# Layer 1 of a four-layer FFN kernel: the router's columns are pooled together with x, and the pooling's steps are reordered

## The reference, cut to what matters

```
attn_in = tanh(x @ W1 + b1)                  # (2, 1024, 64)
scores  = attn_in @ v                        # (2, 1024)
mask    = prefix, suffix, or all but itself, by prompt_type_ids[b]
p       = softmax(where(mask, scores, -1e30))          # (2, 1024, 1024)
z       = (p @ x) / count(mask)              # pooled rows
logits  = z @ Wr + br                        # (2, 1024, 8)
expert  = argmax(logits);  gate = softmax(logits)[expert]
out     = x + gate * FFN_expert(z)
```

## Time and profile before

| what | us |
|---|---|
| runs | 1240.93, 1246.62, 1247.62 |
| the profiled execution | 1239.08 |
| its span | 1237.2 |
[...]
| TensorE matmul busy | 1078.8 |
| VectorE busy | 931.1 |
| ScalarE busy | 647.5 |
| GpSimd busy | 505.1 |

### The profile page before, as it was taken

How to read it: one execution, slowest core, us unless ns; L and a number is a source line. 1 busy time by engine, 2 the same in 40 slices (tenths; PEclk the granted TensorE clock), 3 DMA queues, 4 the chain that set the end, 5 groups by cost and what they waited for, 6 DMA issues and landing times.

```text
span 1237.2 us, 25849 instructions
## 1 busy us (share of the span) xinstructions
PE 1078.8 (87%) x7880; PEld 1004.0 (81%) x7880; DVE 931.1 (75%) x1603; ACT 647.5 (52%) x1370; POOL 505.1 (41%) x345
## 2 busy tenths in 40 slices
PE   6689867999999999999997666999868968989896
PEld 4478857999999999999995446999758966778785
DVE  6766795888888888888865856887547866767695
ACT  3335315767667677676744436676246735323221
POOL 5000013778887888887851004453116750000000
PEclk8799987999999999999996777999889988999898
DMA  6300227676777777777633115764346854030202
GB/s 181 118 21 4 76 85 258 187 244 206 253 233 224 244 224 243 229 224 256 211 63 77 35 52 222 286 215 148 113 162 196 269 163 158 30 99 23 91 14 69
DMA packets 82621, 191.91 MB, mean 155 GB/s; under 512 B 16882, under 2 KB 57602, under 8 KB 70274
## 3 DMA queue, kind: packets, MB, share of 16 engines
q1 hardware_dynamic: 60642, 151.01, 35.7%
q0 software_dynamic: 21920, 40.21, 13.3%
HBM read 158.01 MB, written 33.18 MB: 155 GB/s over the span
## 4 chain that ended last, share of the span: by engine, by line
PE 71%; DVE 13%; issue 6%; DMA 5%; ACT 2%; SPq 1%; DVEq 0%; POOL 0%; POOLq 0%; ACTq 0%
PE ps L804 22%; PE ps L805 22%; PE ps L806 22%; PE ps L933 2%; DVE hidden_lo L1752 2%; DMA w_raw<-z_rows,slot_rows 1%; DMA z_tok<-in_L_w 1%; PE ps L816 1%; DMA y_rows<-w_raw,slot_rows 1%; DVE featA_lo L1752 1%; DVE featB_lo L1752 1%; DVE x_tok L2087 1%; DMA z_tok<-y_rows 1%; DVE w_lo L1752 1%; DVE z_tok L2483 1%
## 5 line engine op out<-in xcount | busy, mean ns | idle before, releaser
L1493 ACT ACTIVATE hidden_f<-ps,b_block 128x256 f32<-128x256 f32 x432 | 222.2, 514 | 170.5 <-PE ps L806 170.4
L694 POOL DMA_INDIRECT x_tok<-z_gate_rows,slot_rows x76 | 208.9, 2749 | 233.1 <-DVE slot_rows L1921 158.4
L1494 ACT ACTIVATE hidden_hi<-ps,b_block 128x256 fp32r<-128x256 f32 x432 | 224.5, 520 | 0.0
L1752 DVE TENSOR_TENSOR hidden_lo<-hidden_f,hidden_hi 128x512 fp32r<-128x512 f32 x284 | 183.9, 691 | 30.4 <-ACT hidden_hi L1494 15.3
L804 PE MATMUL ps<-w_hi,featA_hi 128*128 128x256 f32 (+1 forms) x624 | 179.2, 287 | 8.9 <-ACT hidden_hi L1494 4.0
L804 PE MATMUL ps<-featB_hi,hidden_hi 128*128 128x256 f32 x616 | 176.0, 286 | 3.4 <-DVE hidden_lo L1752 3.4
L805 PE MATMUL ps<-w_lo,featA_hi 128*128 128x256 f32 (+1 forms) x624 | 178.3, 286 | 0.0
L806 PE MATMUL ps<-w_hi,featA_lo 128*128 128x256 f32 (+1 forms) x624 | 178.2, 286 | 0.0
L805 PE MATMUL ps<-featB_lo,hidden_hi 128*128 128x256 f32 x616 | 173.8, 282 | 0.0
L806 PE MATMUL ps<-featB_hi,hidden_lo 128*128 128x256 f32 x616 | 172.8, 280 | 0.0
L722 POOL DMA_INDIRECT x_rows<-w_raw,slot_rows x76 | 126.6, 1666 | 35.5 <-issue 21.9
(11 more groups left out here) (463 smaller groups left out, 2937.7 us busy)
## 6 DMA issues: line engine op xcount, KB each, us to landing
scratch<-in_L_w SPq DMA_DIRECT2D x48, 1024.0 KB, 5.2
z_tok<-in_L_w SPq DMA_DIRECT2D x29, 1024.0 KB, 7.4
x_tok<-in_L_w SPq DMA_DIRECT2D x19, 1024.0 KB, 4.9
b_block<-in_L_ffn_b POOLq DMA_DIRECT2D x60, 128.0 KB, 4.2
z_tok<-y_rows SPq DMA_DIRECT2D x12, 512.0 KB, 5.5
z_tok<-in_L_w SPq DMA_DIRECT2D x12, 512.0 KB, 4.8
scratch<-in_L_w SPq DMA_DIRECT2D x12, 512.0 KB, 4.1
z_rows<-z_tok SPq DMA_DIRECT2D x8, 512.0 KB, 2.9
```

What stands on the lines that cost most here:

```text
L694: gp.indirect_dma_start(XBL[L][:, k, tt, :], None, ZD if L else ZD0, bass.IndirectOffsetOnAxis(ap=TOK[:, q * BTT + tt:q * BTT + tt + 1], a ...
L1493: act.activation(HF[:, f // 2, part], ps, func, bias=b1)
L1494: act.activation(HTh[:, k, f // 2, part], ps, func, bias=b1).then_inc(s_hhi[L], 1)
L1752: return nc.vector.tensor_tensor(out, full, hi.bitcast(F32), ALU.subtract)
```

## The change

- `L1_ffn_Wr` (256 by 8) is no longer loaded at the start. It is loaded beside the conditioning's W1 into the same tile, so that each of the two weight slices has 72 columns instead of 64. `router_split(1)` is gone; `cond_split` covers the 8 more columns. There is one DMA fewer in the first list and one more after it.
- The conditioning's matmuls give 72 partitions: 64 for tanh and 8 for x @ Wr. The four chunks use four PSUM banks (4 to 7), so TensorE no longer waits for a bank. ScalarE follows each tanh with a copy of the 8 partitions into `HF`.
- After the scores TensorE turns the 8 partitions back (16 small transposes into bank 6). VectorE (`router_columns`) splits them into 8 more columns of `XRh` and `XRl`: `PW` becomes 266.
- `XRh` and `XRl` are cut in two: chunks 0 to 2 in `TBh` and `TBl`, chunk 3 in `W2h` and `W2l`. VectorE itself rounds chunks 0 and 1 before the scans; ScalarE rounds chunks 2 and 3 after it has copied both batch rows' scores, and VectorE subtracts them inside batch row 0's pooling (`rows_lo(2)`, `rows_lo(3)`).
- In the pooling the lo part `E1l` comes before `args(b, 0)` instead of after it. `normalize` multiplies the 8 pooled router columns by the reciprocal, straight into the logits' place.
- The turn of z, the logits' matmuls and their turning back are gone on all three engines; the softmax reads the logits from `SC`.

```diff
-                    last = mm3(PS[0:A0, 4 + c % 2, :], W1h[:, 1, w], W1l[:, 1, w], TAh[:, k, c * CH:(c + 1) * CH],
+                    last = mm3(PS[0:A1R, 4 + c, :], W1h[:, 1, w], W1l[:, 1, w], TAh[:, k, c * CH:(c + 1) * CH],
...
+            for n in range(NT):
+                last = nc.tensor.transpose(PS[:, 6, n * 8:(n + 1) * 8], HF[A0:A1R, n // TPC, n % TPC * P:(n % TPC + 1) * P],
+                                           ident[A0:A1R, A0:A1R])
+            last.then_inc(s_lg, 1)
             pe.wait_ge(s_sc_sb, B)
-            pe.wait_ge(s_xr, 1 + NC)
             for b in range(B):
+
+                pe.wait_ge(s_xr, 4 + 2 * b)
...
             pe.wait_ge(s_z1, NT)
-            transposes("z1", Z, lambda c: None, lambda c: logits_t(1, c))
-            logits(1)
             ranks(1)
...
-                act.activation(XRh[:, c * TPC:(c + 1) * TPC, 0:D], X[:, c * TPC:(c + 1) * TPC, :],
-                               ACT.Copy).then_inc(s_act, 1)
+                act.activation(HF[0:A0, c, :], PS[0:A0, 4 + c, :], ACT.Tanh, bias=CB1[:, 0:1])
+                act.activation(HF[A0:A1R, c, :], PS[A0:A1R, 4 + c, :], ACT.Copy).then_inc(s_chf, 1)
...
+            for c in (2, 3):
+                act.activation(xr_chunk(XRh, c), X[:, c * TPC:(c + 1) * TPC, :], ACT.Copy).then_inc(s_act, 1)
...
+            for c in (0, 1):
+                link(nc.vector.tensor_copy(xr_chunk(XRh, c), X[:, c * TPC:(c + 1) * TPC, :]))
+                rows_lo(c)
+
+            def router_columns():
+                dve.wait_ge(s_lg, 2)
+                n0 = 0
+                for x, y in zip(XRh, XRl):
+                    n = x.shape[1]
+                    r = PS[:, 6, n0 * 8:(n0 + n) * 8].rearrange("p (t e) -> p t e", e=8)
+                    link(nc.vector.tensor_copy(x[:, :, TBW:PW], r))
+                    last = lo(y[:, :, TBW:PW], r, x[:, :, TBW:PW])
+                    n0 += n
+                last.then_inc(s_xr, 1)
...
-                nc.vector.reciprocal(SM[:, 2, bs], SM[:, 4, bs]).then_inc(s_den, 1)
+                link(nc.vector.reciprocal(SM[:, 2, bs], SM[:, 4, bs]))
+
+                nc.vector.tensor_tensor(SC[:, 0, 0:NT * 8].rearrange("p (t e) -> p t e", e=8)[:, bs, :],
+                                        PS[:, h * TPC:(h + 1) * TPC, TBW:PW],
+                                        SM[:, 2, bs].unsqueeze(2).broadcast_to([P, TPC, 8]), ALU.mult).then_inc(s_den, 1)
 
             scans(0)
             for b in range(B):
                 carry_in(b)
+                if b == 0:
+                    router_columns()
                 row_maxima(b)
-                args(b, 0)
                 dve.wait_ge(s_phigh, phigh("in", b))
                 lo(E1l[:, b], E1a[:, b], E1h[:, b]).then_inc(s_plow, 1)
+                args(b, 0)
                 carry_out(b)
                 args(b, 1)
                 weights_lo(b, 0)
+                if b == 0:
+                    dve.wait_ge(s_act, 1)
+                    rows_lo(2)
...
                 weights_lo(b, 1)
-                if b + 1 < B:
-                    scans(b + 1)
+                if b == 0:
+                    dve.wait_ge(s_act, 2)
+                    rows_lo(3)
+                    scans(1)
                 normalize(b, 0)
                 normalize(b, 1)
-            transposes("z1", TAh, TAl)
+            dve.wait_ge(s_den, 2 * B)
             top1(1)
```

More of the change, by code:

```diff
@@ L54 @@
 LC = B * SEQ // P
-PW = D + 2
+TBW = D + 2
+PW = TBW + 8
+A1R = A0 + 8
 NCAR = 2 * TPB
@@ L84, in build, with xr, xr_chunk @@
         W2l = sb("w2_lo", [P, 2, FB * D], F32R)
+        XR3C = 3 * TPC * PW
+        XRh, XRl = ([x[:, 0:XR3C].rearrange("p (t w) -> p t w", w=PW),
+                     y[:].rearrange("p a b -> p (a b)")[:, 0:TPC * PW].rearrange("p (t w) -> p t w", w=PW)]
+                    for x, y in ((TBh, W2h), (TBl, W2l)))
+        def xr(x, n):
+            return x[n // (3 * TPC)][:, n % (3 * TPC), :]
+        def xr_chunk(x, c):
+            return x[c // 3][:, c % 3 * TPC:c % 3 * TPC + TPC, 0:D]
         HF = sb("hidden_f32", [P, FB, CH])
@@ L151, in build @@
         RW = [GR if L == 2 else 8 if L < 2 else E3 for L in range(4)]
[L152 to L154 removed]
+        Rr, Rh, Rl = ([None if L == 1 else sb(f"router_{n}{L}", [P, KD, RW[L]], dt) for L in range(4)]
+                      for n, dt in (("raw", F32), ("hi", F32R), ("lo", F32R)))
         WG = sb("wg", [8, 3 * GR])
@@ L245, in build @@
         s_craw = sem("cond_raw")
[L246 removed]
+        CRAW = [16 * n for n in (2 * B, 2 * B + 3, 5 * B + 3, 6 * B + 3)]
         s_csplit = sem("cond_split")
@@ L1322, in _ @@
                 for n in range(TPB):
-                    last = mm3(PS[0:NCAR, 7, 0:PW], E1h[:, b, n, :], E1l[:, b, n, :], XRh[:, b * TPB + n, :],
-                               XRl[:, b * TPB + n, :], n == 0, n == TPB - 1)
+                    last = mm3(PS[0:NCAR, 7, 0:PW], E1h[:, b, n, :], E1l[:, b, n, :], xr(XRh, b * TPB + n),
+                               xr(XRl, b * TPB + n), n == 0, n == TPB - 1)
                 last.then_inc(s_sums, 1)
@@ L1710, in _ @@
                 pooled(b, 1)
-            transposes("z1", TAh, lambda c: logits_t(1, c))
             exps(1, NT * 8)
@@ L2593, in _ @@
             next(masks)
-            for n in (1, 3):
-                router_split(n)
+            router_split(3)
             norm(3)
@@ L2687, in _, with rows_lo @@
             transposes("x1", TAh, TAl)
-            nc.vector.tensor_copy(XRh[:, :, D:D + 2], ONE[:, 0:2].unsqueeze(1).broadcast_to([P, NT, 2]))
-            link(nc.vector.tensor_scalar(XRl[:, :, D:D + 2], ONE[:, 0:2].unsqueeze(1).broadcast_to([P, NT, 2]),
-                                         0.0, None, ALU.mult))
-            dve.sem_inc(s_xr, 1)
-            for c in range(NC):
-                dve.wait_ge(s_act, c + 1)
-                lo(XRl[:, c * TPC:(c + 1) * TPC, 0:D], X[:, c * TPC:(c + 1) * TPC, :],
-                   XRh[:, c * TPC:(c + 1) * TPC, 0:D]).then_inc(s_xr, 1)
+            for x, y in zip(XRh, XRl):
+                n = x.shape[1]
+                nc.vector.tensor_copy(x[:, :, D:TBW], ONE[:, 0:2].unsqueeze(1).broadcast_to([P, n, 2]))
+                last = nc.vector.tensor_scalar(y[:, :, D:TBW], ONE[:, 0:2].unsqueeze(1).broadcast_to([P, n, 2]),
+                                               0.0, None, ALU.mult)
+            last.then_inc(s_xr, 1)
+            def rows_lo(c):
+                lo(xr_chunk(XRl, c), X[:, c * TPC:(c + 1) * TPC, :], xr_chunk(XRh, c)).then_inc(s_xr, 1)
+            for c in (0, 1):
[4 more added lines that the diff above has]
+                n0 = 0
+                for x, y in zip(XRh, XRl):
+                    n = x.shape[1]
+                    r = PS[:, 6, n0 * 8:(n0 + n) * 8].rearrange("p (t e) -> p t e", e=8)
+                    link(nc.vector.tensor_copy(x[:, :, TBW:PW], r))
+                    last = lo(y[:, :, TBW:PW], r, x[:, :, TBW:PW])
+                    n0 += n
+                last.then_inc(s_xr, 1)
             def row_of(b):
```

46 lines of the change are left out of this document (23 added, 23 removed).

## The result

| | before | after |
|---|---|---|
| runs on the same chip, median (lowest to highest), us | 1242.41 (1240.93 to 1247.62), 7 runs | 1235.95 (1235.2 to 1237.64), 7 runs |
| the profiled execution, its span | 1239.08, 1237.2 | 1235.93, 1234.1 |
| mean granted TensorE clock | 0.926 | 0.925 |

The ratio of the runs is 0.9937 with a 95% interval of 0.9918 to 0.9956, that is 7.8 us faster (the ratio goes by all the runs; the two medians alone are 6.5 us apart). Two more timings of the same kernel, beside other runs of before, gave 0.9914 (0.9890 to 0.9937) and 0.9916 (0.9888 to 0.9944), that is 10.7 and 10.5 us. The forecast was 1235, from 1228 to 1240.

What follows compares the result with a forecast made beforehand. The chain up to layer 1's softmax, read link by link, was taken as the bound: 13.4 us removed, pooling ending 2.2 us later, softmax 11.2 us earlier. From the runs' median of 1246.62 that gave 1235 us, range 1228 to 1240.

Steps and rivals of the forecast that it cites:

- Removed: Between last pooling matmul and softmax: 14.50 us of division, turns and router matmuls shrink to 1.1 us, 13.4 us gained.
- (a): Scores on TensorE: no more waits for a PSUM bank between conditioning chunks, ending 0.4 us earlier; bounds 0 to 0.6.
- (b): After the scores: 16 small transposes on TensorE at the lower clock add 1.9 us; bounds 1.16 and 3.4.
- (c): VectorE's split of the router's columns before the maxima: 0.95 us, bounds 0.8 and 1.3; maxima start 2.15 us later.
- (d): Pooling: `E1l` before `args(b, 0)` frees TensorE's first sum 1.06 us earlier in both batch rows.
- (e): ScalarE's roundings of chunks 2 and 3, before its first exponentials, are hidden by 2 us.
- (f): `rows_lo(2)`, 1.23 us, fits VectorE's 1.6 us gap before the carries, some 0.5 us spare; otherwise up to 1.2 shows.
- (g): `rows_lo(3)` before VectorE's second scans adds 1.14 us on the chain; bounds 0 and 1.23.
- (h): Batch row 0's divisions, between scans and second carries: two multiplications and linked reciprocals add 0.55 us; bounds 0.3 and 0.8.
- (i): Pooling matmuls of 266 columns instead of 258 add 0.35 us per pooling; bounds 0 and 0.7 for both.
- rival 1: Clock stays full through the scores, maxima start 1.85 us earlier than in the sum: gain 13.1 us, time 1233.5; chance 0.08.
- Added work dear: Transposes, split and other added VectorE work before the softmax cost 3.4 us more: gain 7.8, time 1239; chance 0.08.

Runs made afterwards that it cites:

- the two delays: Changed kernel plus six or twelve useless linked VectorE instructions (4.4 or 8.8 us) before the softmax: 1240.09 us (0.9956 of before) and 1245.26 us (0.9997).
- g_turn_kept: Changed kernel, but z is turned again and the logits are made the old way after the pooling: 1247.17 us, 1.0016 of before.
- c_old_order: Changed kernel with `args(b, 0)` before `E1l` again in the pooling: 1233.56 us, 0.9900 of before.
- e_all_on_vector: Changed kernel with VectorE rounding and subtracting all four chunks of x ahead of the first scans: 1232.08 us, 0.9878 of before.
- h_delay6: Changed kernel with six useless linked VectorE instructions, 4.4 us in all, between last division and softmax: 1240.09 us, 0.9956 of before.
- j_warm_row1: Changed kernel with four useless TensorE matmuls before batch row 1's first sum: one run, 1233.13 us beside 1244.51 of before.

## Why the prediction was right, step by step

- **What bounds it.** Confirmed. The chain from scores to softmax sets the end of the stage. That a microsecond there is about one of the program, the two delays and `g_turn_kept` show within their intervals.
- **The sum.** 11.2 us was forecast at the softmax, 11.16 measured. The median of the three timings, 7.8, 10.7 and 10.5 us, is close to it. Three things in this hit are luck. The lead rests on one trace of before: against its second one, where the clock fell later, it is 9.9 us. The time of 1235 for 1235.95 is a base too high (1246.62, the median of three runs, where seven gave 1242.41) less a gain too large for this timing (11.2 for 7.8). And within the sum two errors cancel: the second row's sum started 0.85 us earlier than forecast, and its pooling, from +46.96 to +59.62, took 1.24 us more than before's (+45.94 to +57.36), where 0.35 was taken.
- **Removed.** 13.4 forecast, 13.6 by `g_turn_kept`; from the last pooling matmul's end to the softmax 719.71 - 718.62 = 1.1 us, as said.
- **(a)** The scores end at 681.26, +22.25, against +23.06: 0.8 us earlier where 0.4 was taken, outside its bounds (0 to 0.6). The moment at which the clock fell is in these numbers too; the two traces of before alone differ by 2.8 us there. The term itself is better read where the scores start, 670.55 or +11.54 against 671.49 or +11.89: 0.35 us, as forecast. The other 0.45 came because the clock fell at +15.1 for +14.9, with more of the scores already done.

```profile
670.55 1.05 PE L1322 MATMUL ps<-cond_v,hidden_f 64*128 64x1 f32 x8
```

- **(b)** 1.87 us for 1.9. **The wait**: 1.73 us for 1.7.
- **(c)** 683.99 - 683.18 = 0.81 us for 0.95. The maxima start at +24.98 against +23.40: 1.58 us later, not 2.15, of which 0.4 is (a) and 0.14 the split.
- **(d)** Confirmed by `c_old_order` at the start of the sums (1.04 us in row 0, and 1.64 in row 1 for the 2.1 of both rows), refuted as time at the softmax: 1.0 of 1.64 us arrived, because the matmuls that started earlier ran at the lower clock (0.50, 0.22 us apart). The sum starts at +28.24 against +27.71, 0.53 later, for 1.09.
- **(e), (f)** Hidden as said; the gap before the carries is 0.40 us for "some 0.5". In batch row 0 the clock rises at +32.11 in before and +32.17 in after, so that row's pooling shows no such loss.
- **(g)** `rows_lo(3)` is on the chain with 695.75 - 694.61 = 1.14 us, as said. Second scans +36.74 against +35.15.
- **(h)** 701.26 - 700.23 = 1.03 us against 699.79 - 699.24 = 0.55 in before: 0.48 for 0.55. The second row's sum starts at +46.96 against +45.94, 1.02 later for 1.87; the missing 0.85 is (a), (c), 0.07 here and some 0.2 in the first row's pooling. The instruction behind the divisions in before:

```profile
699.79 0.14 DVE L2709 COPY carry_max<-z_tok 128x7 f32<-128x7 f32 x1
```

- **(i) is the mis-sized term.** Width was costed at 0.35 us per pooling on the silent assumption that the clock takes the same course. In before it rose at +49.11, inside the second row's sum; in all three traces of after it rose at +52.4 to +52.9, when the sum was over or all but over. The pooling so lost 0.9 us beyond the 0.35 of its width. The later start did this, not the width: `e_all_on_vector`, as wide, took 11.64 us for that pooling where after took 12.66 and before 11.42, and four useless matmuls ahead of after's own sum brought the rise back. The start had moved from 13.8 to 14.8 us after the first rise. A sum of durations cannot show this; the spacing of the matmuls or the granted clock by windows does.
- **The rest at nothing.** No sign of a cost in the trace: layer 1's loop took 143.59 against 143.12 us, and softmax to slot rows 14.37 against 14.30, so ScalarE's last scaled rows are hidden as said.
- **Rivals.** The clock staying up through all the scores (rival 1) happened in no trace. It fell at +14.7 to +15.3 in eleven, the three of after among them, and only at +16.4 to +16.9 in three others: before's own second one, `g_turn_kept` and `h_delay6`, whose first sums start at +26.65, +26.04 and +25.93. So it differs from run to run, and this part of the rival's course already gave `h_delay6` 2.3 us, where 1.85 was forecast for the whole of it. "Added work dear" is refuted: every added term but (i) was at or below its value. A DMA in routing's place is refuted by the waits and by 11.20 us of lead at layer 1's add-back. An extra step is refuted: layer 1's loop has the same length.
- **The clock among the scores.** It was taken to fall there as it had before, where its mean over this stretch was 0.61, and it did. The moment of the fall moved by some 2 us between two traces of one kernel, from +15 to +17; what sets it, no run shows. In after TensorE was busy 11.07 of 11.50 us in the stretch of the fall, at a mean clock of 0.59:

```profile
672.00:683.50 11.50, 11.07 (x48) 7.63 (x46) 5.96 (x11) 3.62 (x7) 0.00 (x0) 0.59 0.00 1
683.50:700.00 16.50, 11.35 (x72) 9.17 (x72) 15.96 (x27) 5.75 (x10) 0.00 (x0) 0.77 0.00 0
```

VectorE, at 15.96 of 16.5 us against 13.61 in the earlier trace rows, is now what the first pooling waits for. `e_all_on_vector`, which takes two subtractions out of that stretch, is ahead at the softmax, 1.2 us by this and 1.0 by the clock.

## What to carry to other kernels

When a linear step follows a linear reduction, carry its few columns through the reduction: here 8 columns, 3% wider matmuls, 1.9 us of small transposes and 0.8 us of splitting removed a 13 us chain of turns. Judge a local gain at the first point where both kernels must pass (here the softmax) and test by a known delay, with runs enough, how much of it reaches the end; two traces of the changed kernel differed by 4.9 us in an untouched stage. Where TensorE's bursts are short, compare the granted clock of each burst before and after, since an earlier start may only buy more matmuls at the lower level (here 1.64 us at the start of the second sum, against `c_old_order`, were 1.0 at the softmax).

## What the runs showed of the hardware that was not expected

- The second row's clock rose 17.0 to 17.2 or 20.4 to 20.6 us after the first row's, in fourteen traces, with nothing between. The first row's rose at +31.9 to +32.4 for sums that started anywhere from +26.6 to +29.3, and at +30.1 to +30.7 in the three traces whose clock had fallen later. What fixes these moments is open.
- The granted clock fell from 0.99 or 1.00 to 0.50 or 0.51 while TensorE was fed almost without a gap. It did so among the scores' matmuls (in after TensorE was busy 2.10 of 2.10 us before the fall and 7.00 of 7.00 behind it), and in the middle of the pooling's matmuls in `j_warm_row1` (6.50 of 7.00 us busy before it, clock 0.99) and `g_turn_kept` (2.75 of 3.10 us, clock 1.00), after 7.0 and 3.3 us at the full level.
- Layer 2's block loop varied from 79.55 to 85.02 us over fourteen traces. In the five of before and after TensorE's waits for gathers in it lay between 10.4 and 13.1 us. One trace's late stretches say little about a change 200 us earlier.
